# Adding expert results to the output inside the scatter, tile by tile, instead of reading two planes back at the end

## The reference, cut to what matters

```python
x = x + gnn(xn) + mix(xn)                     # "acc" in the kernel
tokens = layernorm(x)
probs = softmax(tokens @ router_w.T)
rw, re = top_k(probs, 2); rw = rw / rw.sum()  # two experts for each node
out = tokens
for e in range(8):
    h = gelu(tokens @ w1[e] + b1[e]); y = h @ w2[e] + b2[e]
    out = out + combine[:, e:e + 1] * y       # combine: rw at the two experts, else 0
return x + out
```

## Time and profile before

| | us |
|---|---|
| median of 3 runs (786.92 to 793.68) | 791.93 |
| the profiled execution | 797.36 |
| its span, first to last instruction | 795.6 |
| last expert scatter issued, in the span | 749.15 |

### The profile page before, as it was taken

The page is one execution under the profiler, slowest core; times in us unless marked ns, Lnnn a source line. Parts: engine busy times, 40 slices in busy tenths (PEclk is TensorE's granted clock), DMA queues, the critical chain, the costliest instruction groups (busy, mean ns, idle before and its releaser), DMA issues.

```text
span 795.6 us, 13909 instructions
## 1 busy us (share of the span) xinstructions
PE 596.3 (75%) x5198; PEld 526.3 (66%) x5198; DVE 511.6 (64%) x1077; ACT 347.0 (44%) x623; POOL 134.5 (17%) x132
## 2 busy tenths in 40 slices
PE   0699582862999999999599999988850399999400
PEld 0254241752999999997499999888750399998300
DVE  6767998468999999954841111396761177877424
ACT  0026464280777777750131111322320399898200
POOL 1000000000000000000000000007786256655500
PEclk9879986795999999999799999998855599999855
DMA  7999999002134444000027686302332345554295
GB/s 181 263 283 283 284 282 345 4 1 93 64 158 207 208 208 208 2 1 1 1 86 327 270 350 236 134 1 69 82 86 78 89 124 155 157 147 136 53 248 188
DMA packets 80159, 121.17 MB, mean 152 GB/s; under 512 B 8574, under 2 KB 68771, under 8 KB 78430
## 3 DMA queue, kind: packets, MB, share of 16 engines
q1 hardware_dynamic: 70621, 107.03, 44.4%
q0 software_dynamic: 9472, 13.27, 5.2%
HBM read 50.00 MB, written 72.21 MB: 154 GB/s over the span
## 4 chain that ended last, share of the span: by engine, by line
PE 52%; DVE 24%; DMA 7%; issue 5%; ACT 4%; POOL 3%; SPq 1%; DVEq 1%; another core or an unknown queue 0%; ACTq 0%; POOLq 0%
PE psB L1218 20%; DVE hot L677 7%; PE psB L1370 4%; PE psD L1274 3%; PE psC L1124 3%; PE psC L1218 3%; PE psA L1136 3%; DMA back<-expert_out 3%; POOL expert_slots L568 3%; PE psD L1136 2%; DMA acc<-in_x_dram 2%; PE psC L1382 1%; PE psD L1382 1%; PE psA L1358 1%; DVE qkv L726 1%
## 5 line engine op out<-in xcount | busy, mean ns | idle before, releaser
L1218 PE MATMUL psB<-hs,counts 125*128 125x256 f16 x1600 | 210.8, 275 | 3.3 <-DVE hs L791 2.7
L1218 PEld LDWEIGHTS psB<-hs,counts 125*128 125x128 f16 x1600 | 173.0, 140 | 4.6 <-issue 2.8
L677 DVE TENSOR_TENSOR hot<-iota_j,places 128x2048 bf16<-128x2048 bf16 x128 | 155.2, 1223 | 15.4 <-PE psA L1136 9.8
L560 POOL IOTA row_of<- 128x25 f32 x1 | 0.2, 237 | 503.5 <-PE psC L1218 503.5
L1413 ACT CAST counts<-psA 128x1000 f16<-128x1000 f32 x64 | 63.3, 989 | 39.6 <-PE psA L1136 39.6
L1136 PE MATMUL psA<-hot 128*128 128x125 bf16 x512 | 50.8, 224 | 36.8 <-DVE hot L677 34.0
L574 POOL DMA_INDIRECT expert_out<-y,to_row x64 | 67.2, 1050 | 61.3 <-DVE y L1060 48.5
L568 POOL DMA_INDIRECT expert_slots<-rows,place x50 | 63.1, 1263 | 50.3 <-issue 48.2
L1136 PEld LDWEIGHTS psA<-hot 128*128 128x128 bf16 x512 | 39.2, 100 | 47.0 <-DVE hot L677 36.2
L1413 ACT CAST counts<-psD 128x1000 f16<-128x1000 f32 x64 | 63.6, 993 | 13.9 <-PE psD L1136 13.9
L851 DVE TENSOR_TENSOR sum_both<-psB,sum_both 128x256 f32<-128x256 f32 x32 | 13.5, 421 | 74.6 <-ACT sum_both L1475 74.6
(11 more groups left out here) (284 smaller groups left out, 1076.2 us busy)
## 6 DMA issues: line engine op xcount, KB each, us to landing
expert_slots<-zeros SPq DMA_DIRECT2D x8, 3536.0 KB, 30.2
kept_counts<-counts SPq DMA_DIRECT2D x6, 4000.0 KB, 11.8
counts<-kept_counts SPq DMA_DIRECT2D x6, 4000.0 KB, 13.0
xs<-expert_slots SPq DMA_DIRECT2D x32, 272.0 KB
back<-expert_out SPq DMA_DIRECT2D x5, 1120.0 KB
w_raw<-in_L_ffn_w_dram SPq DMA_DIRECT2D x2, 2048.0 KB, 7.9
acc<-in_x_dram SPq DMA_DIRECT2D x1, 2800.0 KB
out_dram<-acc SPq DMA_DIRECT2D x5, 560.0 KB
```

Source lines behind the costliest of these rows:

```text
L677: v.tensor_tensor(hot[:, slot].rearrange("p g w n s -> p (g w) n s"), iota_j[:, :, :].unsqueeze(1).to_broadcast([P, 2 * pairs, P, PAIR]), ...
L1218: m = pe.matmul(sum_bank(g, d), counts5[0:PT, buf, a, d, :], hs2[0:PT, a, :, :].rearrange("p q f -> p (q f)"), start=a == 0 and first, sto ...
```

## The change

`expert_out`, `back` and the adds on DVE are gone. The output is first stored as `acc` + tokens, chunk by chunk, while the router works (after `acc_tok_ok`). The scatter of `y` then goes straight to the output's rows with `compute_op=ALU.add`: the DMA adds each row to what the output holds. A slot row now holds the node's number only once over (the last 8 values are all the same), without a plane.

Two experts may add to the same node, and such adds must not be in flight together. So tile t may be added only when the tiles before it that are of another expert have landed. That holds for t - 1 and t - 2; tile t - 3 must have landed in any case. DVE makes a table `tab_landed`: the count that the semaphore `added` of tile t - 1 (and t - 2) must have reached, 32 higher where the expert differs. SP walks over the tiles, loads a slot tile five ahead (now 6 buffers `xs`), waits for tile t - 3, reads the two values, waits for them, and then counts up `may_add`, for which POOL waits before the tile's two adds. So that no wait is for zero, POOL first issues three adds with all rows left out (`no_row`).

```diff
-X_BUFS = 4
-SKIP = 8191
-assert SKIP >= 2 * NODES
+X_BUFS = 6
+SKIP = 4095
+assert SKIP >= NODES
+Y_BUFS = 3
...
+            for c in range(C):
+                sp.wait_ge(acc_tok_ok, c + 1)
+                for lo, hi in ((0, 112), (112, PT)):
+                    sp.dma_start(out_v[lo:hi, c], acc_v[lo:hi, c]).then_inc(stored, 16)
             sp.wait_ge(table_ok, 2)
             sp.wait_ge(spread, 16 * 2 * SLOTS)
-            for n in range(MOE_TILES):
+            def load_slots(n):
...
-            for b in range(3):
-                sp.wait_ge(returned[b], 32 * ((MOE_TILES - b + 2) // 3))
...
-            for c in range(C):
-                for lo, hi in ((0, 112), (112, PT)):
-                    sp.dma_start(back[lo:hi, c], back_v[lo:hi, c]).then_inc(back_in[c], 16)
...
+            for n in range(X_BUFS - 1):
+                load_slots(n)
+            sp.wait_ge(tab_landed_ok, 2)
+            for t in range(MOE_TILES):
+                if t + X_BUFS - 1 < MOE_TILES:
+                    load_slots(t + X_BUFS - 1)
+                sp.wait_ge(added[t % Y_BUFS], 16 + 32 * (t // Y_BUFS))
+                backs = range(1, min(t, Y_BUFS - 1) + 1)
+                landed = [sp.value_load(tab_landed[0:1, back - 1, t:t + 1], min_val=16, max_val=16 + 32 * MOE_TILES) for back in backs]
+                for back, value in zip(backs, landed):
+                    sp.wait_ge(added[(t - back) % Y_BUFS], value)
+                    sp.nop()
+                sp.nop().then_inc(may_add, 1)
...
+            pool.wait_ge(stored, 32 * C)
+            for b in range(Y_BUFS):
+                pool.indirect_dma_start(out[:, :], bass.IndirectOffsetOnAxis(no_row[0:PT, 0:1], 0), acc[0:PT, b, :], None,
+                                        bounds_check=NODES - 1, oob_is_err=False, compute_op=ALU.add).then_inc(added[b], 16)
             for t in range(MOE_TILES):
+                pool.wait_ge(may_add, t + 1)
                 pool.wait_ge(gate_row_ok, t + 1)
                 for q in range(2):
                     pool.wait_ge(y_ok, 2 * t + q + 1)
-                    pool.indirect_dma_start(expert_out[:, :], bass.IndirectOffsetOnAxis(to_row[:, t % 3, q:q + 1], 0), y[:, t % 3, q, :], None,
-                                            bounds_check=2 * NODES - 1, oob_is_err=False).then_inc(returned[t % 3], 16)
+                    pool.indirect_dma_start(out[:, :], bass.IndirectOffsetOnAxis(to_row[:, t % Y_BUFS, q:q + 1], 0), y[:, t % Y_BUFS, q, :], None,
+                                            bounds_check=NODES - 1, oob_is_err=False, compute_op=ALU.add).then_inc(added[t % Y_BUFS], 16)
...
+            for back in range(1, Y_BUFS):
+                v.scalar_tensor_tensor(tab_landed[:, back - 1, back:MOE_TILES], landed_f[:, 0:MOE_TILES - back], 16.0, other_e[:, back - 1, back:MOE_TILES],
+                                       ALU.add, ALU.add).then_inc(tab_landed_ok, 1)
...
-                    if t >= 3:
-                        v.wait_ge(returned[t % 3], 32 * (t // 3))
+                    if t >= Y_BUFS:
+                        v.wait_ge(added[t % Y_BUFS], 16 + 32 * (t // Y_BUFS))
...
-                v.tensor_tensor(a, a, back[0:PT, c, 0], ALU.add).then_inc(first_back_ok, 1)
...
-                v.tensor_tensor(a, a, back[0:PT, c, 1], ALU.add).then_inc(out_ready, 1)
```

More of the change, by code:

```diff
@@ L398, in gps_layer @@
         y_ok = sem("y_ok")
-        returned = [sem(f"returned{b}") for b in range(3)]
-        back_in = [sem(f"back_in{c}") for c in range(C)]
-        out_ready = sem("out_ready")
+        added = [sem(f"added{b}") for b in range(Y_BUFS)]
+        no_row_ok = sem("no_row_ok")
+        may_add = sem("may_add")
+        tab_landed_ok = sem("tab_landed_ok")
         acc_tok_ok = sem("acc_tok_ok")
-        first_back_ok = sem("first_back_ok")
         merged = sem("merged")
@@ L523, in _ @@
                 sp.dma_start(xs[:, n % X_BUFS], slots[bass.ds(at, SLOT), :].rearrange("(p q) f -> p q f", q=2)).then_inc(slots_in[n % X_BUFS], 16)
-            for b in range(3):
-                sp.wait_ge(returned[b], 32 * ((MOE_TILES - b + 2) // 3))
-            back_v = expert_out.rearrange("(j c p m) f -> p c j (m f)", j=2, p=PT, m=W)
-            out_v = out.rearrange("(c p m) f -> p c (m f)", p=PT, m=W)
-            for c in range(C):
-                for lo, hi in ((0, 112), (112, PT)):
-                    sp.dma_start(back[lo:hi, c], back_v[lo:hi, c]).then_inc(back_in[c], 16)
[L531 to L535, removed]
+            for n in range(X_BUFS - 1):
[12 more added lines that the diff above has]
+            for b in range(Y_BUFS):
+                sp.wait_ge(added[b], 16 + 32 * len(range(b, MOE_TILES, Y_BUFS)))
         IN_W = 16 * 14
@@ L569, in _ @@
                                                 None).then_inc(spread, 16)
+            pool.wait_ge(no_row_ok, 1)
+            pool.wait_ge(stored, 32 * C)
+            for b in range(Y_BUFS):
+                pool.indirect_dma_start(out[:, :], bass.IndirectOffsetOnAxis(no_row[0:PT, 0:1], 0), acc[0:PT, b, :], None,
+                                        bounds_check=NODES - 1, oob_is_err=False, compute_op=ALU.add).then_inc(added[b], 16)
             for t in range(MOE_TILES):
+                pool.wait_ge(may_add, t + 1)
                 pool.wait_ge(gate_row_ok, t + 1)
@@ L952, in router @@
                 st.did(v.tensor_tensor(picked[0:PT], pick[0:PT], share[0:PT].unsqueeze(3).to_broadcast([PT, 2, W, EXPERTS]), ALU.mult))
[L953 to L954 removed]
+                v.tensor_copy(rows[0:PT, c, :, DIM + EXPERTS:ROW], row_of[0:PT, W * c:W * c + W].unsqueeze(2).to_broadcast([PT, W, ROW - DIM - EXPERTS])).then_inc(weights_in_row, 1)
                 st.wait()
@@ L1028, in _ @@
             v.tensor_scalar(tab_r[:], tile_at_r[:], float(EXPERTS * REGION), None, ALU.min).then_inc(table_ok, 1)
+            st.did(v.memset(other_e[:], 1.0))
+            st.wait()
+            for back in range(1, Y_BUFS):
+                st.did(v.tensor_tensor(other_e[:, back - 1, back:MOE_TILES], tile_e[:, back:MOE_TILES], tile_e[:, 0:MOE_TILES - back], ALU.not_equal))
+            st.wait()
+            for back in range(1, Y_BUFS):
+                st.did(v.tensor_scalar(other_e[:, back - 1, :], other_e[:, back - 1, :], 32.0, None, ALU.mult))
+            st.wait()
+            for back in range(1, Y_BUFS):
+                v.scalar_tensor_tensor(tab_landed[:, back - 1, back:MOE_TILES], landed_f[:, 0:MOE_TILES - back], 16.0, other_e[:, back - 1, back:MOE_TILES],
+                                       ALU.add, ALU.add).then_inc(tab_landed_ok, 1)
             v.wait_ge(table_ok, 2)
```

32 lines of the change are left out of this document (14 added, 18 removed).

## The result

| | before, us | changed, us |
|---|---|---|
| median of 20 runs each | 792.32 (786.92 to 795.96) | 786.79 (782.57 to 788.25) |
| the profiled execution | 797.36 | 787.56 |
| its span | 795.6 | 785.8 |
| start of tile 0's first scatter or add | 641.05 | 641.38 |
| start of the last one | 749.15 | 779.62 |

The ratio is 0.9918 [0.9903, 0.9932]: 5.5 us less by the medians, where 30 were forecast. The tail shrank by 40.3 us (46.4 - 6.2, rounded) as the change intends, and the expert stage with the empty tiles grew from 108.1 to 138.2 us, 30.1 of which were not there before. The forecast had 11 for that, and 3 for stalls.

What follows compares the result with a forecast made beforehand. Bound by the engines' pace in the expert stage, then a 44.4 us tail. Start 641.05 + groups 107.8 + empty tiles 13.0 + 0.4 = 762.3 against 795.6; less 3 for stalls, 30 us saved: median 762, range 746 to 786.

Steps and rivals of the forecast that it cites:

- near no change: Whole run: measured time within about 1%, 8 us, of the kernel before; chance 0.04.
- What bounds the kernel before: Expert stage at the engines' pace, 3.3 us a tile; then a 44.4 us tail existing only because results lie in planes.
- The stores, the adds without rows, the DVE table, SP's walk at nothing: Router's time and expert stage: all hidden; adds without rows 3.8 us, SP's walk about 2.4 us a tile.
- L = 4.0: Expert stage: us from a tile's second add's start to its landing, between 2.4 (adding free) and 5.1 (full read first).
- The formula G(n): Expert stage: n tiles of one expert take, landing to landing, 1.2 us + (2n-1) DMA distances + one flight.
- p = 1.38: POOL: us between two DMAs, now 1.27; taken halfway between 1.27 and 1.49, the latter from the token scatter's issue.
- 0.4 from the last landing to the end: End of the program: some 0.4 us from the last DMA's end to the end of the span.
- 3 us for stalls: Expert stage: 3 us charged of the present 5.4 us of stalls, slack and the sixth slot buffer removing some.
- (d): POOL's issue doubles to 1.94 us, distance 2.24: 13 us more, median 805; chance 0.14 with (c).
- (a): Expert stage: add free, new wait nearly hidden, stage keeps 97.8 us; 43.7 us less, median 748; chance 0.15.
- (b): Expert stage: distance 1.49 and flight 5.1 us, both upper ends; 15 us less, median 777; chance 0.12, including somewhat beyond.
- (c): DMA engines do a scatter's rows one after another, flight 10.1 us: 36 us more, median 828; chance 0.14 with (d).

Runs made afterwards that it cites:

- the third experiment: Changed kernel with plain scatters into two planes that are not read back and no waits at changes of expert: 755.09 us, ratio 0.9503 to the kernel before.
- the constants: Changed kernel with constants for SP's walk, POOL itself waiting for landings, SP holding slot loads back: 787.19 us, ratio 0.991 to the kernel before.
- the first experiment: Changed kernel with plain scatters instead of adds to the output, every wait kept: 773.43 us, ratio 0.9729 to the kernel before.
- half-row run: Planes kernel without waits, each DMA taking 64 of 128 rows, a tile's first scatter adding and its second plain: 752.61 us, one run.

## Why the prediction was wrong

The direction was right and nearly all of the tail went, as forecast; the size was not right: 5.5 us less instead of 30, a median of 786.79 against 762, just above the range. A change of under 8 us had the heading "near no change" and a chance of 0.04. Its steps:

- **What bounds the kernel before.** Held: the tail fell from 46.4 to 6.2 us, and the third experiment (40.3 us under the kernel before by the medians, some 3.5 of them from six slot buffers) puts a bound on everything that the planes cost.
- **The stores, the adds without rows, the DVE table, SP's walk at nothing.** Held. The first slot load starts at 625.27, in the earlier trace rows at 625.48, and tile 0 at 641.38 instead of 641.05. The adds without rows took 6.0 us instead of 3.8, hidden. That the walk costs nothing is borne out by the constants (0.991 against 0.9906, and 0.76 us from landing to start without it).
- **L = 4.0.** Held roughly, 3.5 to 3.8. The upper end of 5.1 was not needed, and the 2.4 of the free add, counted from the start of the issue, did not come: the next expert starts 4.4 us in the mean after an add's start, against 3.4 after a plain scatter's. Of that 1.0 us 0.57 is the longer issue, and some 0.4 is left for the flight. The rule of "Collectives: The Full Stack" in the Trainium skill, section "Stop ④ — SDMA + CCE: where bytes move and the add happens", that the add is free in the stream, is therefore nearly met by the flight in this trace; the 0.57 us on POOL it does not speak of.
- **The formula G(n).** Held: with p = 1.85 and L = 3.7 it gives 14.2 for three tiles and 21.6 for five; measured 677.53 to 691.21, 13.7, and 655.73 to 677.53, 21.8. The hop from landing to start was 0.8, where 1.2 was charged. But it held because POOL was the bound. For the first experiment, with plain scatters, it fails: 9.0 us to tile 2's second start, 43 distances of 1.28 and eight changes of 3.6 make some 93 us for 28 tiles, and 109.6 were measured. So a stage bound by the other engines pays a further price for the waits that the formula lacks, and had an add's issue been as cheap as assumed, the forecast need not have come true.
- **p = 1.38: this is the step that failed.** It read "halfway, since the DMA has one more address per row to be given", with 1.49 as the upper end. Measured 1.85, outside both ends. The upper end came from the token scatter, a plain DMA over 125 partitions, and says nothing on what an accumulating one costs; no row did. In the formula (2n - 1)p over all groups has the factor 48 (56 DMAs less 8), so 0.47 more is 22.6 us, and POOL needs 3.70 us a tile, over the 3.3 of the engines; L and the hop give back 2.4 and 3.2, which leaves 17.0, and the rows show 125.3 for 28 tiles where 109.0 was forecast, 16.3 more. The empty tiles took 12.9 from first start to last start where 9.7 was forecast, 3.3 more.
- **"0.4 from the last landing to the end" and a 2.1 us landing.** Missed by 3.7: from the last start to the end were 6.2 us. SP has passed its last wait at 782.4, 2.8 us after the last start, but POOL's closing drain goes on until 785.6, 4.4 us after its last issue. In the kernel before the same drain ended at 756.3, hidden by the tail; the cover went with the tail.
- **3 us for stalls.** Not there: the engines' stalls vanish behind POOL.

The sum in spans, before the 3 us of stalls: forecast 762.3, and +0.3 at the start, +16.3, +3.3 and +3.7 make 785.9; measured 785.8. The median moved less than the span (5.5 against 9.8) since the profiled execution of before was 5 us above its median.

Of the rivals, (d), the issue on POOL becoming the bound, was right in kind: it put double the issue, 1.94, and the point from which the change loses at p = 1.98; measured were 1.54 and 1.85, and its formula 694.8 + 51 p gives 789 with that. Its price was reasoned per row ("A row would need double the words"), and against it stood that much of the plain 0.97 is fixed. The half-row run shows that the step itself is mostly not per row. (a) was wrong twice: the add is not free, and the sentence "and so the new wait is nearly hidden" fails by itself, since with plain scatters the wait costs 18.3 us. It took the longer of POOL's G and the engines' pace for the stage; in the first experiment POOL waits for `y` between the changes too, and the stage is longer than either. (b) came nearest among the faster ones (777) by other terms: its L was too long and its p too short. (c) is excluded: L is 3.7.

## What to carry to other kernels

When an operation moves to another engine's issue, ask first what one issue of the new kind costs there, and if no row shows it, put the upper end at the point where that engine becomes the bound, not at the nearest plain row. Where the issuing engine is the bound, a wait for a landing between groups costs its full latency each time, so count changes times (landing + hop). Where the other engines are the bound, do not take the wait for hidden: here it cost 18.3 us. Before replacing a tail, shorten it in place: here six slot buffers and stores that overlap the readback gave as much, within the intervals, as removing the readback.

## What was unexpected of the hardware

- The issue of an indirect DMA on POOL: 0.97 us plain and 1.54 with an add at 128 rows; 0.94 and 1.41 at 64; 1.19 and 2.0 over 125 partitions. The price is nearly that of the DMA, not of the rows, and 128 partitions are cheaper than 125.
- The software queue's packets went from 9472 to 16864 with the adds at the same bytes (13.27 and 13.29 MB). With the token scatters over 128 partitions instead of 125 they fell from 16864 to 12864.
- POOL's drain at the end lasts until 4.4 us after its last issue with adds and 6.2 with plain scatters (the kernel before), which shows only where nothing else ends later.
